# Causal attention with sixteen columns of ones per head: the softmax sums are moved to their rows by DMAs of the sync engine

## The reference, cut to what matters

```python
k = jnp.repeat(k, rep, axis=2)                      # rep = 4 query heads share one key/value head
v = jnp.repeat(v, rep, axis=2)
scores = jnp.einsum('bthd,bshd->bhts', q, k) / np.sqrt(HD)
scores = jnp.where(causal[None, None], scores, -jnp.inf)
attn = jax.nn.softmax(scores, axis=-1)
out = jnp.einsum('bhts,bshd->bthd', attn, v)
gate = jax.nn.sigmoid(out @ Wg + bg)
out = (out * gate).reshape(batch, seq, DIM)
x = x + out @ Wo + bo
```

## Time and profile before

| | us |
|---|---|
| three runs | 1872.42, 1872.81, 1869.1 |
| the profiled execution, time of its own | 1870.13 |
| its span, first to last instruction | 1868.3 |
| mean granted TensorE clock | 0.929 of full speed |
| this attention, from the first scores to the last value product | about 618 to 806 |

### The profile page before, as it was taken

The page is one execution under the profiler, slowest core; times in us unless marked ns, Lnnn a source line. Parts: engine busy times, 40 slices in busy tenths (PEclk is TensorE's granted clock), DMA queues, the critical chain, the costliest instruction groups (busy, mean ns, idle before and its releaser), DMA issues.

```text
span 1868.3 us, 26191 instructions
## 1 busy us (share of the span) xinstructions
PE 1613.8 (86%) x9225; PEld 1109.1 (59%) x9225; DVE 1096.8 (59%) x2172; ACT 859.4 (46%) x1379; POOL 804.2 (43%) x769
## 2 busy tenths in 40 slices
PE   5953999968976899983996887999999999997988
PEld 3443999955755333363995566555555655563774
DVE  4761465567977355442446598667666777644335
ACT  2422355313336998742452564444454354431463
POOL 3053211213445454423004374666776576745106
PEclk9775999979988899986998998899999999998999
DMA  9613233130000000062112100100010011021454
GB/s 362 241 47 122 81 135 110 53 121 9 1 14 1 1 7 6 7 250 110 48 50 71 49 1 18 58 18 18 18 24 18 7 24 24 1 91 66 134 157 135
DMA packets 68279, 126.41 MB, mean 68 GB/s; under 512 B 9551, under 2 KB 52803, under 8 KB 65464
## 3 DMA queue, kind: packets, MB, share of 16 engines
q1 hardware_dynamic: 60088, 104.56, 16.7%
q0 software_dynamic: 8064, 20.19, 3.3%
HBM read 72.26 MB, written 44.89 MB: 63 GB/s over the span
## 4 chain that ended last, share of the span: by engine, by line
PE 68%; DVE 13%; POOL 6%; issue 5%; DMA 4%; ACT 3%; SPq 0%; POOLq 0%; DVEq 0%; ACTq 0%
PE psum L167 64%; DMA arena<-xb 2%; POOL arena L871 2%; DVE arena L172 1%; DVE arena L1744 1%; POOL xb L1058 1%; POOL arena L1867 1%; DVE arena L188 1%; PE psum L683 1%; DVE arena L1979 1%; ACT arena L1621 1%; DVE arena L1183 1%; PE psum L1370 1%; POOL xb L866 1%; PE psum L207 1%
## 5 line engine op out<-in xcount | busy, mean ns | idle before, releaser
L167 PE MATMUL psum<-arena 128*128 (+15 forms) x5084 | 1019.6, 434 | 96.9 <-DVE arena L1728 16.6
L167 PEld LDWEIGHTS psum<-arena 128*128 128x128 f32 (+4 forms) x5084 | 583.7, 173 | 419.5 <-issue 279.3
L167 PE MATMUL psum<-rounded 128*128 128x256 f32 (+9 forms) x3072 | 525.0, 336 | 10.0 <-DVE rounded L2336 3.5
L167 PEld LDWEIGHTS psum<-rounded 128*128 128x128 f32 (+5 forms) x3072 | 404.0, 184 | 140.6 <-issue 46.0
L2507 POOL TENSOR_TENSOR arena<-arena 128x1024 f32<-128x1024 f32 (+1 forms) x111 | 262.6, 2366 | 88.8 <-ACT arena L2465 80.0
L2416 DVE TENSOR_REDUCE arena<-psum 128x1 f32<-128x512 f32 x256 | 169.5, 681 | 112.4 <-PE psum L167 109.9
L2465 ACT ACTIVATE arena<-psum 128x1024 f32<-128x1024 f32 x144 | 147.2, 1024 | 98.4 <-PE psum L167 97.0
L1621 ACT ACTIVATE arena<-psum,arena 128x1024 f32<-128x1024 f32 x128 | 134.5, 1116 | 21.5 <-PE psum L167 20.3
L871 POOL DMA_INDIRECT arena<-yb,arena x48 | 46.0, 957 | 211.1 <-DMA yb<-arena 197.6
L1211 POOL DMA_INDIRECT yt<-arena x40 | 39.8, 996 | 182.5 <-DVE arena L1174 177.1
L919 DVE SCALAR_TENSOR_TENSOR rounded<-arena,rounded 128x540 fp32r<-128x540 f32 (+1 forms) x96 | 81.8, 885 | 33.4 <-ACT rounded L1120 32.3
(11 more groups left out here) (267 smaller groups left out, 1859.5 us busy)
## 6 DMA issues: line engine op xcount, KB each, us to landing
arena<-in_w SPq DMA_DIRECT2D x8, 2048.0 KB, 8.5
arena<-xb SPq DMA_DIRECT2D x70, 128.0 KB, 2.3
yb<-arena SPq DMA_DIRECT2D x70, 128.0 KB, 1.7
arena<-in_w1u SPq DMA_DIRECT2D x4, 2048.0 KB, 14.5
rounded<-rounded SPq DMA_DIRECT2D x64, 128.0 KB, 2.2
xb<-arena SPq DMA_DIRECT2D x3, 2048.0 KB, 16.0
xb<-arena SPq DMA_DIRECT2D x2, 2064.0 KB, 31.6
arena<-xb SPq DMA_DIRECT2D x8, 516.0 KB
```

What stands on the lines that cost most here:

```text
L167: return e.matmul(o, l, r, start=start, stop=stop, skip_group_check=True)
```

## The change

The value tiles get 32 columns per head and no overlap: 16 of values and 16 of the number 2. So the value product writes twice the sum to all of the rows 32r+16 to 32r+31. The product with "sel", DVE's copy of its result and the semaphore s_spc are gone, and so is the constant. Instead SP waits for s_oes and issues four DMAs per chunk, each of which moves the 16 rows of sums of one head from OES to the rows 32r to 32r+15 of got(c); each adds 16 to s_spr. The other rows of got(c) are set to 1 by POOL ahead of time (s_blank1). The value tiles now lie at oAW, so the load of in_aw's third part moves on SP from the end of sp_ffn0 to a place behind the last value product.

```diff
-    ("desc", 16), ("caus", 128), ("cos", 64), ("sin", 64), ("sel", 128), ("dsel", 128), ("eoff0", 8), ...
+    ("desc", 16), ("caus", 128), ("cos", 64), ("sin", 64), ("dsel", 128), ("eoff0", 8), ...
...
@@ sp_ffn0, at its end
-            e.dma_start(view(oAW, 2048), d["aw"][2]).then_inc(s_aw[0], 16)
...
-        VX = view(o + 10752, NT, 4, 17)
+        VX = view(oAW, NT, 4, 32)
...
-        va = lambda t, r: view(o + 10752 + 68 * t + 17 * r, 32)
+        va = lambda t, r: VX[:, t, r, :]
...
@@ sp_ffn1
-            for c in PACKED:
+            for u, kept, c in sorted([(n + 2, 1, c) for c, n in enumerate(ENDS)] + [(u, 0, c) for u, c in AT_GATE.items()]):
+                if kept:
+                    e.wait_ge(s_oes, c + 1)
+                    e.wait_ge(s_blank1, c + 1)
+                    if c:
+                        e.wait_ge(s_spr, 64 * c)
+                    for r in range(4):
+                        e.dma_start(got(c)[32 * r:32 * r + 16, :], OES[c % 2][32 * r + 16:32 * r + 32, :]).then_inc(s_spr, 16)
+                    continue
+                if c not in PACKED:
+                    continue
                 e.wait_ge(s_go, c + 1)
                 for r in range(4):
                     e.dma_start(got(c - 2)[32 * r + 16:32 * r + 32, :], got(c)[32 * r:32 * r + 16, :]).then_inc(s_pk[c // 8], 16)
             e.wait_ge(s_ae, STEPS1[-1])
             e.wait_ge(s_apv, len(UNITS))
+            e.dma_start(view(oAW, 2048), d["aw"][2]).then_inc(s_aw[0], 16)
             e.dma_start(f1_B1.rearrange("p e c -> p (e c)"), d["b11"]).then_inc(s_wm, 16)
...
@@ pe_value1
             if kts[0] == 0 and c >= 2:
-                e.wait_ge(s_spc, c - 1)
+                e.wait_ge(s_oes, c - 1)
...
@@ pe_ffn1
-                if u in AT_SPREAD:
-                    c = AT_SPREAD[u]
-                    e.wait_ge(s_oes, c + 1)
-                    mm(e, psum[:, 6 + c % 2, :], cst("sel"), OES[c % 2], True, True).then_inc(s_spr, 1)
...
@@ dve_ffn1
                 if u in AT_SPREAD:
                     c = AT_SPREAD[u]
-                    e.wait_ge(s_spr, c + 1)
-                    if c < 14:
-                        e.tensor_copy(got(c), psum[:, 6 + c % 2, :]).then_inc(s_spc, 1)
-                        e.wait_ge(s_spc, c + 1)
-                        settle(e, dve, e.reciprocal(got(c), got(c)))
-                    else:
-                        settle(e, dve, e.reciprocal(got(c), psum[:, 6 + c % 2, :]))
+                    e.wait_ge(s_spr, 64 * (c + 1))
+                    settle(e, dve, e.reciprocal(got(c), got(c)))
                     e.tensor_tensor(got(c), OES[c % 2], got(c), ALU.mult).then_inc(s_nrm, 1)
...
@@ pool_ffn1
-            settle(e, pool, e.memset(view(o + 10752, 1104), 0.0))
             e.memset(view(o + 5088, 60, 64)[:, :, 48:64], 0.0)
-            e.memset(VX[:, :, :, 16:17], 1.0).then_inc(s_vx, 2)
+            e.memset(VX[:, :, :, 16:32], 2.0).then_inc(s_vx, 2)
...
+            e.wait_ge(s_pj, NT)
+            e.wait_ge(s_l, NT)
             for u, (b, j, qc, kts) in enumerate(UNITS):
+                if u - 1 in ENDS or u == 1:
+                    c = ENDS.index(u - 1) + 1 if u > 1 else 0
+                    if c < 16:
+                        e.memset(got(c), 1.0).then_inc(s_blank1, 1)
```

More of the change, by code:

```diff
@@ L38 @@
     ("ident", 128), ("hm", 8), ("tri", 128), ("ones", 128), ("rst32", 512), ("rst16", 128),
-    ("desc", 16), ("caus", 128), ("cos", 64), ("sin", 64), ("sel", 128), ("dsel", 128), ("eoff0", 8), ("iota", 48), ("nhalf", 16)])
+    ("desc", 16), ("caus", 128), ("cos", 64), ("sin", 64), ("dsel", 128), ("eoff0", 8), ("iota", 48), ("nhalf", 16)])
 NSML = _layout(SML, [
@@ L1308, in build @@
         s_oes, s_spr, s_nrm, s_gt = sem("o_out"), sem("sums_spread"), sem("o_divided"), sem("gate_prod")
-        s_spc = sem("spread_out")
+        s_blank1 = sem("spread_blank")
         s_gx2, s_go = sem("o_gate_tanh"), sem("o_gated")
@@ L3077, in constants @@
     put("sin", np.sin(fr).reshape(128, 64))
-    put("sel", 2.0 * (p[:, None] == p[None, :] // 32 * 32 + 16))
     put("dsel", p[:, None] % 32 == p[None, :] // 32 * 8 + p[None, :] % 32 // 16 * 4)
```

## The result

The changed kernel took 1886.01 us in the median (1884.64 to 1888.40, four runs), the kernel before 1872.20 beside it: a ratio of 1.0078, 95% interval 1.0061 to 1.0096. So the change costs some 14 us, about double of what was forecast, and 1886 lies outside the forecast range. The direction was right.

A forecast was written before the change was run, and what follows sets the result against it. PE (20.09 us busy) and ACT (19.86) were taken to bound each 21.50 us pair. Terms -0.2 + 2.3 + 4.5 - 0.3 = +6.3 us gave 1877.4 us; own range 1874 to 1880, 8 in 10 1868.5 to 1882.

The forecast's parts named there:

- the missing 17 us of PE work: Selection products leave PE, 16 x 1.05 us; worth 0.94 us per turn where ACT sets the pace.
- the memset: GpSimd's 0.584 us memset for the next even chunk delays unit 11's masks: +0.58 us per turn.
- The DMA chain: Four DMAs per chunk: about 3.95 us from copy to reciprocal, before 1.95 (even) or 3.50 (odd); near 5.6 behind packing.
- the sum of the turns: From one pair to the next +0.94 us, with packing +0.44, the first about 0; four turns +2.3 us.
- The overlap: DVE's two-input operations and GpSimd's masks exclude each other: +1.3 us per turn, 0.8 where the chunk is packed behind.
- a sign that I had named: In the profile after, PE's busy time in the attention less by 17 us.
- the product turns and what follows: Pairs 5 and 6, DVE's chain on the path: +2.7 us at pair 5's gate, +4.7 in pair 6, +4.5 at the end.
- chunk 9's spread: Pair 5: chunk 7's late gate makes SP issue packing as chunk 9's copy ends, adding up to 1.6 us.
- the pair behind gives little back: After pair 6: chunk 14's gate has the same longer chain, so +4.7 us becomes +4.5 at the last value product.
- A: Even chains slip between the masks, exclusion costs nothing, only the product pairs lose, +2.5 us: 1871.7 us, chance 0.22.
- B: ACT's idle time goes in all seven turns, -9 us, product pairs give back +2.5: 1864.6 us, chance 0.12.
- C: Clock falls in both product pairs behind PE's longer waits and stays low one unit more: 1880.7 us, chance 0.16.

The follow-up runs named there:

- the shuffle with delays: Kernel with the stream shuffle plus GpSimd memsets of 512 unused columns and one more DVE reciprocal for chunks 2, 4, 6, 8: 1865.77 us, ratio 0.9957.
- the run without anything extra among the masks: Changed kernel without memsets, even chunk's reciprocal two units later, its multiplication reading values from PSUM; four DMAs per chunk kept: 1870.69 us, ratio 1.0000.
- the shuffle: Changed kernel with sums moved by one DVE stream shuffle from OES to got(c), without DMAs of sums or memsets: 1856.60 us, ratio 0.9921.
- the run with the late even chunk: Changed kernel with DVE's reciprocal and multiplication of an even chunk two units later in its program: 1876.57 us, ratio 1.0029.

## Why the prediction was wrong

**The mechanisms that stood.** The ordinary turn follows GpSimd's row of masks, and the missing 17 us of PE work were worth 0.9 a turn (21.5 to 20.6 us, forecast 0.94). VectorE's late operations and the memset fall into that row. The DMA chain is on the path in the product turns. The tiles and the moved load cost nothing that can be told. At the last chunk the time from copy to reciprocal went from 4.24 to 3.85 us (forecast 3.95).

**The step that failed first: the sum of the turns.** "So a turn from one pair to the next: -0.94 + 0.58 + 1.3 = +0.94." Measured were +2.24, +2.30 and +1.09. Two of its terms hold: 0.9 comes back and the memset costs 0.5 to 0.6 (21.2 against 20.6). The overlap was put too high, 1.3 for 0.9. Put together at full clock this is less than forecast: 22.15 us with both delays (turn 3 of the shuffle with delays) against 21.53, +0.6. What was missing is the clock, a term that the sum puts at nothing. By this difference, which is an estimate across two kernels, it is 1.6, 1.7 and 0.5 us in turns 1, 2 and 3, 3.8 of the +5.4 by which the four turns together came out (forecast +2.3). I had the clock as a rival, but only behind the long waits of the product turns, because those were the only gaps that I looked for. In turns 1 and 2 it stood at 1.2 GHz for 7 us each behind waits of 1.03 and 0.73 us in a row.

The same term hides a sign that I had named. PE's busy time in the attention was to be less by 17 us, and it is less by 1 (170.0 to 168.95 us from 618 to the last copy), because slower matmuls fill the rest. In the run without anything extra among the masks it is 160.4.

**The second: the product turns and what follows.** "+4.5 at the last value product" against +6.47 - 0.38 + 3.19 = +9.3. The first half was right in kind: chunk 9's spread was behind chunk 7's packing, and PE's stall grew by 2.3 us in turn 4 and by 1.8 in turn 5. Missed was again the clock, which fell in both turns:

```profile
723.10:751.30 28.20, 24.98 (x174) 10.26 (x170) 13.76 (x15) 20.12 (x21) 11.62 (x12) 0.94 0.02 5
751.30:778.00 26.70, 23.50 (x172) 9.92 (x168) 13.58 (x14) 20.10 (x21) 11.60 (x12) 1.00 0.03 7
```

These are the two turns before; now both have 0.89. PE is busy for 23.74 and 24.20 us, and the same work takes 21.7 at full clock, with the shuffle. So slow matmuls are some 4.5 us of the two turns, against 1.5 before, an estimate of up to 3 us more. Missed was also chunk 14: "the pair behind gives little back" had its chain in it as a clause and no number. The stretch behind the last mask turn grew by 3.2 us, its low clock (0.81) included.

**The rivals.** A put the product turns at +2.5, the ordinary ones at -1.4 and the whole at 1871.7. In the run with the late even chunk the product turns are at +2.8, but the five ordinary ones at +1.6 and the whole at 1876.57, so A holds there for one part only. B (PE's relief wins) has its condition in the run without anything extra among the masks: 0.9 to 1.0 us a turn and not 1.3, just enough to pay for the DMAs in the product turns and behind them, and no more. C was the rule that I had weighed and applied in too few places. It names 1880.7, nearer than the forecast, and was still 5 us short.

The Trainium skill (TensorE: Matmul & The Clock Gate, on a second failure mode of the clock gate) describes a kernel whose TensorE idles briefly and often between groups of matmuls, so that its clock goes back and forth between the two levels. The turns at 0.86 agree with it: their single idle pieces were near 1 us.

## What to carry to other kernels

A latency that nobody waits for still moves work. Follow it to the next instruction of that engine which slows the engine on the path, here VectorE's two-operand operations that made GpSimd's mask of 1.28 us last 1.7, and count every wait on PE that grows by it twice: once as itself, and once as a chance that the clock falls. And before sums travel between partitions by DMA (3.9 us by four, 2.7 by one) or by a matmul, see whether the engine that uses them can move them itself: the shuffle took 0.75.

## What the runs showed of the hardware

- A DMA of 112 rows of 2 KB within SBUF landed 2.6 us after its issue in the median (2.6 to 3.7), one of 16 rows 2.0 (1.9 to 3.3); four of the latter cost 2.4 us of issue on SP, so the one with seven times the rows was ready 1.2 us sooner.
- VectorE's two-operand operations of 0.69 us took up to 1.82, and GpSimd's mask of 1.28 up to 1.75, where they met.
- A memset on GpSimd beside VectorE's operations kept its 0.52 us (at 734.08 in the changed kernel, inside a two-operand operation that lasted from 732.92 to 734.68).
- Once fallen, the granted clock stayed at 0.50 of full speed for about 7 us (turns 1 and 2 of the changed kernel) or about 3.5 us (its turn 3, and the turns at 0.92 of the other runs), with PE busy nearly all of that time, before it came back.
